# A pairwise-interaction tower on one core: the table look-ups of tile 5 are held until the first four tiles have been transposed

## What is computed

```python
e = jnp.stack([tbl_f[ids[:, f]] for f in range(32)], axis=1)      # 1024 x 32 x 64
p, q = e[:, ROW], e[:, COL]                                       # the 496 pairs
z = jnp.sum(jnp.einsum('bpj,ipj->bpi', p, kernel) * q, axis=-1)   # 1024 x 496
h = jnp.concatenate([z, dense_ctx], axis=1)
h = jnp.maximum(h @ W_top1 + b_top1, 0.0)
h = jnp.maximum(h @ W_top2 + b_top2, 0.0)
y = h @ W_top3
```

## Time and profile before

| | |
|---|---|
| median of 3 runs | 493.63 us (490.99 to 494.14) |
| the profiled execution | 490.83 us, its span 489.1 us |
| PE busy | 445.8 us, 91% of the span |
| DVE busy | 303.2 us, 62% |
| ACT busy | 260.7 us, 53% |
| POOL busy | 232.3 us, 48% |
| mean TensorE clock granted | 0.972 of full speed |

### The profile page before, as it was taken

The page is one execution under the profiler, slowest core; times in us unless marked ns, Lnnn a source line. Parts: engine busy times, 40 slices in busy tenths (PEclk is TensorE's granted clock), DMA queues, the critical chain, the costliest instruction groups (busy, mean ns, idle before and its releaser), DMA issues.

```text
span 489.1 us, 10184 instructions
## 1 busy us (share of the span) xinstructions
PE 445.8 (91%) x3421; PEld 249.8 (51%) x3421; DVE 303.2 (62%) x293; ACT 260.7 (53%) x1874; POOL 232.3 (48%) x251
## 2 busy tenths in 40 slices
PE   8469989989998999799998998899999899999997
PEld 4136545545555455355654554555554555564443
DVE  7316567776766677677656775776776878771000
ACT  6026674756656767663566657545586668101122
POOL 6715656566555565556555555556655640000000
PEclk9759999989999999999999999899999999999999
DMA  6145654121018111211121112111121101000000
GB/s 170 42 135 159 195 163 121 21 66 21 19 21 193 23 24 21 66 21 23 20 64 23 25 20 68 20 20 22 24 63 24 21 20 45 0 3 0 0 1 1
DMA packets 18266, 24.31 MB, mean 50 GB/s; under 512 B 6387, under 2 KB 11767, under 8 KB 17958
## 3 DMA queue, kind: packets, MB, share of 16 engines
q1 hardware_dynamic: 10406, 15.64, 10.9%
q0 software_dynamic: 7808, 8.01, 8.4%
HBM read 19.44 MB, written 0.00 MB: 40 GB/s over the span
## 4 chain that ended last, share of the span: by engine, by line
PE 82%; another core or an unknown queue 6%; DVE 6%; issue 3%; ACT 2%; POOL 0%; POOLq 0%; DVEq 0%; ACTq 0%
PE u_ps L688 36%; PE u_ps L709 13%; PE z_ps L722 11%; PE u_ps L769 6%; PE z_ps L728 6%; DVE prod L605 5%; PE t_ps L642 4%; PE u_ps L789 3%; PE u_ps L695 1%; PE z_ps L664 1%; DVE prod L608 1%; DVE pass_prod L616 0%; PE u_ps L631 0%; ACT prod L522 0%
## 5 line engine op out<-in xcount | busy, mean ns | idle before, releaser
L417 POOL DMA_INDIRECT nat<-tbl,ids_sb x244 | 231.2, 947 | 166.7 <-issue 59.0
L605 DVE TENSOR_TENSOR prod<-u_ps,rows 128x1024 f32<-128x1024 f32 x184 | 218.2, 1220 | 106.8 <-PE u_ps L688 53.3
L502 ACT ACTIVATE pass_prod<-pass_prod 128x64 f32<-128x64 f32 x896 | 214.6, 243 | 38.0 <-DVE pass_prod L616 30.4
L688 PE MATMUL u_ps<-rows,k_sb 64*128 64x256 f32 x1472 | 194.3, 395 | 16.6 <-DVE prod L605 9.3
L688 PEld LDWEIGHTS u_ps<-rows,k_sb 64*128 64x128 f32 x1472 | 133.3, 187 | 102.8 <-issue 46.4
L502 ACT ACTIVATION_READ_ACCUMULATOR pass_prod<-pass_prod 128x1 f32 x896 | 169.5, 189 | 3.6 <-issue 3.6
L616 DVE TENSOR_TENSOR pass_prod<-u_ps,nat 128x1024 f32<-128x1024 f32 x56 | 68.1, 1217 | 23.9 <-PE u_ps L709 19.0
L709 PE MATMUL u_ps<-k_sb,rows 64*128 64x256 f32 x448 | 65.1, 408 | 5.7 <-DVE prod L605 3.5
L722 PE MATMUL z_ps<-prod,sel 128*32 128x512 f32 x512 | 69.9, 612 | 0.0
L490 ACT ACTIVATE rows<-t_ps 128x512 f32<-128x512 f32 (+1 forms) x38 | 19.5, 514 | 90.0 <-remote 55.3
L709 PEld LDWEIGHTS u_ps<-k_sb,rows 64*128 64x128 f32 x448 | 43.0, 194 | 22.9 <-DVE prod L605 8.3
(11 more groups left out here) (50 smaller groups left out, 95.8 us busy)
## 6 DMA issues: line engine op xcount, KB each, us to landing
by_self<-rows SPq DMA_DIRECT2D x32, 128.0 KB
nat<-tbl,ids_sb POOLq DMA_INDIRECT x244
k_sb<-kern SPq DMA_DIRECT2D x3, 768.0 KB
k_sb<-kern SPq DMA_DIRECT2D x2, 640.0 KB
k_sb<-kern SPq DMA_DIRECT2D x1, 1152.0 KB
k_sb<-kern SPq DMA_DIRECT2D x2, 512.0 KB
rows<-w SPq DMA_DIRECT2D x1, 1024.0 KB
rows<-tbl SPq DMA_DIRECT2D x4, 224.0 KB
```

The lines of the kernel that those rows point to most:

```text
L417: pool.indirect_dma_start(nat_of(m, n)[:, h * EMBED:(h + 1) * EMBED], None, tables[f], bass.IndirectOffsetOnAxis(ids_sb[:, col:col + 1], 0 ...
L502: op = nc.scalar.activation(of, of, ACT.Copy, accum_out=z_nat[:, b % 2, s, row:row + 1])
L605: nc.vector.tensor_tensor(to, u, by.unsqueeze(1).to_broadcast([P, 2, 2, SIZE]), ALU.mult).then_inc(prod_ready, 1)
L688: op = nc.tensor.matmul(u[:, h, :], k_sb[part, k_of(d), side, :], rows[part, tile, cols_of(b)], start=True, stop=True)
```

## The change

Position 5 (tile 5) gets a wait of its own on POOL: its first gather is issued only once `transposed` is at least 4, that is after positions 0 to 3 (tiles 2, 3, 0 and 1). Nothing else is changed. The gathers of all later positions stand behind it in POOL's order.

```diff
 AHEAD = 30
+IN_STEP = {5: 4}
...
                 if m in BY_PRODUCT:
                     continue
                 b, tile = tile_at(m)
-                if m >= LANES:
+                if m in IN_STEP:
+                    pool.wait_ge(transposed, IN_STEP[m])
+                elif m >= LANES:
                     pool.wait_ge(transposed, m - LANES + 1)
```

## The result

The changed kernel takes 487.87 us, the median of 6 runs (487.33 to 489.39). The kernel before, run beside it, takes 492.95 us, the median of 6 (490.12 to 494.14). The ratio is 0.9913, with a 95% interval of 0.9887 to 0.9939, so the gain is 5.1 us. The forecast was 481 us, a gain of some 12. The result lies in the range, but most of the forecast gain didn't come. The profiled execution took 487.76 us with a span of 486.0; its span is 3.1 us shorter than that of the profiled execution before (489.1).

A forecast was written before the change was run, and what follows sets the result against it. PE was taken to bound the kernel, apart from a hole of some 13 us near the start. Removing it, -13.5, plus 0.7 for the new wait, gave -12.8 us: 480.8 from the median 493.63, said as 481, range 477 to 497.

The forecast's parts named there:

- first hole: Stretch of some 13 us near the start, from 14 to 28 us, where PE is busy only 5.2 us.
- Step (1): Without the first hole tile 3's look-up runs through; `transposed` reaches 4 at 18.0, not 31.55: a gain of 13.5 us.
- the reading: A long unbroken run of gathers holds PE up, a little after five, badly after more than eight.
- Nothing changes: Rival, chance 0.20: the first hole has another cause and stays; 0.6 us slower, 494.2 us.
- step (2): The new wait delays POOL's ninth gather to about 18.3; tile 7 comes late; cost some 0.7 us.
- whole step of one DMA, 1.25 us: Allowance for gathers landing later beside kernel loads: from nothing to 1.25 us.
- Step (4): Behind the first hole PE is busy 24.7 of 26 us, so the gain goes through to the end.
- The hole moves: Rival, chance 0.17: a new long gather run holds PE later; net gain 3 to 5 us, 488.5 us.
- second hole: Hold of PE during the gathers behind the new wait, 28.3 to 38 us, 8 to 10 us lost.
- its threshold: In the moved hole, PE is held from the ninth gather of the run on, at 28.3 us.
- its sign: The moved hole would show as single PE matmuls with 0.7 to 1.5 us between them at 28 to 38 us.
- Two holes for one: Rival, chance 0.17: the first hole stays at 13 us and a second run adds another; 7.6 us slower, 501.2 us.

The follow-up runs named there:

- x7_sp: Kernel before, with the eight gathers of tiles 5 and 6 replaced by plain transfers that SP issues at 11 us (their look-ups left out): 479.43 us, ratio 0.9729.
- x4_more: Kernel before, with four more gathers of rows already there between positions 5 and 6, so the first run is of 21: 497.78 us, ratio 1.0104.
- x11_after: The changed kernel again, unaltered, on the faster kind of chip: 427.53 us against 423.29 of the kernel before, ratio 1.0081.
- x2_late: Changed kernel with its wait one position later, ahead of position 6, so the first run is of twelve gathers: 489.86 us, ratio 0.9935.
- x1_drain: Kernel before, with POOL waiting ahead of positions 5, 6 and 7 until the previous position's gathers have landed: 489.86 us against 492.94, ratio 0.9935.
- x3_both: Changed kernel, with POOL also waiting ahead of positions 6, 7 and 8 until the previous position's gathers have landed: 490.58 us, ratio 0.9961.
- x5_busy: Kernel before, with three small memsets on POOL, each waited for, ahead of positions 5, 6 and 7: 485.19 us against 492.48, ratio 0.9852.
- x16_plain: Kernel before, with every gather from position 8 on a plain transfer (look-ups left out), on the faster kind of chip: 422.74 us, ratio 0.998.
- x18_plain: Kernel before, with every gather from position 5 on a plain transfer (look-ups left out), on the faster kind of chip: 420.47 us, ratio 0.9918.

## Why the prediction was wrong

**Right:** that the first hole is the gathers' doing, and its size. Step (1) gave a look-up of tile 3 ending at 15.8 (16.15), `transposed` at 4 by 18.0 (the transpose of tile 1 ends at 18.50, and the ninth gather starts at 18.77), and 13.5 us for the hole (31.55 - 18.50 = 13.1); x7_sp gained 13.0. One support of the reading doesn't stand: of the eight gaps of PE from 60 us on that the views of the kernel before put down to "issue" (0.59 to 1.84 us), three begin within 0.6 us of the end of a run of gathers, not all eight. The reading came true on the strength of the first hole. "Nothing changes" fell with x4_more and x7_sp: the hole's end follows the end of the gathers, and without them the same code of PE has no hole. The Trainium skill ("Runtime: NRT & Kernel Launch", section "Instruction fetch mechanics") tells of a stall when a taken branch leaves the fetched window; by it the four gathers of x4_more, which change nothing in PE's code, wouldn't have moved anything, and they moved ACT's copy from 27.56 to 30.84.

**Right in kind, too small:** step (2), the new wait's price. Tile 5 was put at 24.1, 1.8 us early. No row of kind A shows it alone, since PE was held there by ACT's copy anyway; on kind B the wait costs some 1.7 us up to tile 7, where 0.7 was taken. The term that was too small is the 1.1 us from the last issue's end to the data being there: in x11_after the last gathers of tiles 5 and 6 end on POOL at 21.69 and 26.68, and PE is let go at 24.24 and 29.29, 2.6 us later each time. The "whole step of one DMA, 1.25 us" that was allowed for contention beside the kernel loads doesn't quite cover it.

**Wrong, and this is the step that failed:** the sum had no term for the second run. Step (4), "so the gain goes through to the end", rested on POOL's and PE's rows from 34 to 60 us, and the same rows were the argument against the rival *The hole moves*: "in before POOL runs from 34.47 to 60 with only short pauses and PE is at 95%". In that stretch the trace of the kernel before has runs of 3, 3, 2, 4 and 5 gathers, with pauses of 0.9 to 2.4 us between them; I read POOL's busy share where the length of its runs was the question. That it is these pauses that let PE's counts through is argued from the experiments with breaks of 2 us; a pause of 1 us wasn't tried on kind A. The term left out is 10.5 us (14.6 us ahead at the end of the first double, 4.1 at tile 6), for the run of twelve that the change itself makes out of nine: 8.0 us of idle time and 2.5 us of matmuls at a lower clock. The clock was also at nothing in the sum on the other side: PE does the first pass and the look-up of tile 4 1.6 us faster at 1.00 than at 0.57, a gain that step (1) didn't count. So the profiled executions give -13.1 - 1.6 + 10.5 + 1.0 = -3.2, to rounding the 3.1 between the spans; the 1.0 is lost between tile 6 and the end.

The rival had put the second hole at 8 to 10 us, from 28.3 to 38, and the time at 488.5; it was there from 24.9 to 36.5, and the median is 487.87. How near this is owes something to luck: the rival counted neither the clock's gain nor its loss. What it had wrong is its threshold, since it isn't the ninth gather that starts the hole, and its sign: it looked for single matmuls with 0.7 to 1.5 us between them, and PE does its pieces whole and then waits for the others' counts. Why PE trickles in the first hole (and in x4_more) and not in the second stays open.

**"Two holes for one"** was right in its premise, that eight gathers are enough to hold a completion (14.76 for a result of about 12.6; x2_late's eight held one until 1.7 us behind the run), and wrong in what ends it: the hole doesn't end by a clock of its own but with the run (x2_late, x4_more), so cutting the run after eight leaves 2 us of the first hole, not 13.

The Trainium skill ("SBUF — State Buffer", section "Who interferes with whom") says that DMA never contends with a compute engine and that PE waits for nobody for SBUF. The runs don't contradict it as a statement on ports, since a matmul of a double is about as long on both kinds of chip (398 and 392 ns); as a reason to expect no effect of POOL's gathers on PE it misleads here, by 13.0 us (x7_sp).

## What to carry to other kernels

On kind A a wait that cuts a long run of GpSimd's indexed gathers moved the run and didn't shorten it (the changed kernel, x1_drain, x3_both): what is queued behind the wait makes the next run. Look at the longest unbroken run on the queue and at when the other engines' counts arrive within it, not at the busy share; three breaks of 2 us, which left runs of 8, 4, 4 and 9 (x5_busy, -7.3 us), did more than one wait of 5.7 us (-5.1, on another chip of the kind). And measure such a change on more than one chip: this one is worth -5.1 us on one kind and +4.2 on the other.

## What the runs showed that I had not expected

**Held completions all through the kernel, on one kind of chip.** After PE's eight matmuls of a double or a pass, one multiplication on DVE follows. Take only those for which DVE stood idle when PE finished, and measure from the end of the eighth matmul to DVE's start. On kind B (x11_after) there are 97 of them, all at 0.05 us, and 76 fall inside a run of gathers, one at its 60th. On kind A, in the traces of the kernel before and of the changed kernel, there are 69: 43 within 0.3 us, and 26 later, by up to 8.9 us. Of the 43 prompt ones 31 fell outside a run and 12 on its first or second gather, none on a third or later. Of the 26 late ones 18 came 0.96 to 1.51 us after the end of a run's last gather; of the other eight, five came while the run still went on, and three 0.3 to 2.6 us behind it. So in these two traces no completion of PE that fell on the third or a later gather of a run was handed over promptly, and most came when the run was over. It isn't without exception: in the seven other traces of kind A, counted in the same way, there are 248, and three that fell on the third or fourth gather of a run of four came at 0.05 us (one in x1_drain, two in x3_both, all between drains). This is counted, not explained; why one chip does it and another doesn't, no run tells.

**The two kinds of chip differ by 68 us in a kernel that PE bounds,** and by 60 in the changed kernel. Group L691 (the doubles) and windows of 100 us of the changed kernel on kind A:

```profile
L691 PE MATMUL u_ps<-rows,k_sb 64*128 64x256 f32 x1472 | 197.6, 398 | 18.5 <-DVE prod L608 14.6
```
```profile
100.00:200.00 100.00, 90.92 (x762) 53.00 (x762) 68.70 (x60) 62.38 (x479) 57.68 (x62) 0.98 0.22 48
200.00:300.00 100.00, 92.64 (x788) 53.44 (x790) 72.22 (x62) 60.01 (x457) 59.24 (x64) 1.00 0.14 29
```

and on kind B (x11_after):

```profile
L691 PE MATMUL u_ps<-rows,k_sb 64*128 64x256 f32 x1472 | 187.1, 392 | 0.0
```
```profile
100.00:200.00 100.00, 97.87 (x894) 61.01 (x896) 79.72 (x69) 68.33 (x525) 65.97 (x71) 0.98 0.24 51
200.00:300.00 100.00, 99.74 (x934) 62.48 (x928) 81.49 (x71) 68.08 (x524) 69.11 (x74) 1.00 0.19 38
```

The granted clock is the same within 0.01, a matmul of a double takes nearly the same time (398 and 392 ns), and PE gets through 1828 matmuls in 200 us on kind B and through 1550 on kind A. The difference is spread over the kernel. It is only in part PE's idle time: by the two pages PE is busy 441.1 of 486.0 us on kind A and 414.9 of 426.2 us on kind B, so of the 60 us between the spans 34 are idle time and 26 are busy time, and what makes the busy time longer with matmuls of the same length no view says. Held completions are one part that can be seen: 25 us of DVE's idle time in the changed kernel is lag of over 0.5 us. That they are the whole of it isn't shown; the runs that would have told (x16_plain, x18_plain) fell on kind B.
